# Graph network layer on one core: part of the x rows gathered by GpSimd beside the chunk loop, 21 chunks of counts instead of 25

## The reference

```python
msg = x[src] + edge_attr                                  # 206250 x 128
agg = segment_sum(msg, dst, num_segments=6250)            # 6250 x 128
h = relu(agg @ W1 + b1) @ W2 + b2                         # 128 -> 256 -> 128
h = (h - mean(h)) * rsqrt(var(h) + 1e-5) * ln_w + ln_b    # over all of h
sub = h - gn_ms * mean(h, axis=0)
h = sub * rsqrt(mean(sub ** 2, axis=0) + 1e-5) * gn_w + gn_b
out = layernorm(x + gelu(h) + x)                          # 6250 x 128
```

## Time and profile before

| | us |
|---|---|
| median of 3 runs | 906.94 (905.07 to 907.28) |
| profiled execution | 911.31 |
| its span, first to last instruction | 909.3 |
| PE busy | 729.4 (80%) |
| DVE busy | 678.4 (75%) |
| ACT busy | 383.4 (42%) |
| POOL busy | 145.4 (16%) |
| granted TensorE clock, mean | 0.959 |

### The profile page before, as it was taken

One profiled execution on the slowest core, in us unless ns is written; L12 is line 12 of the kernel. 1 busy time (PEld: TensorE's weight loads), 2 busy tenths in 40 slices (PEclk: granted clock), 3 DMA queues, 4 the chain that ended last, 5 costly groups with the idle time before them and its releaser, 6 DMA issues.

```text
span 909.3 us, 25887 instructions
## 1 busy us (share of the span) xinstructions
PE 729.4 (80%) x9449; PEld 633.5 (70%) x9449; DVE 678.4 (75%) x1185; ACT 383.4 (42%) x841; POOL 145.4 (16%) x91
## 2 busy tenths in 40 slices
PE   3486569888988888988889988889988889989950
PEld 2464448777877777877777877777877777877830
DVE  5844777877878877878877878877878877844576
ACT  0200034355433555433554433554434554424464
POOL 1210022120221220221120221220221220200000
PEclk9987989899999999999999999999999999999975
DMA  6669973443334443334444334443334444303004
GB/s 173 228 216 361 360 262 99 124 147 115 104 100 121 147 144 116 106 97 125 147 144 114 107 94 128 147 144 112 109 93 130 147 144 113 94 25 141 0 1 141
DMA packets 89477, 123.25 MB, mean 136 GB/s; under 512 B 9029, under 2 KB 85018, under 8 KB 89260
## 3 DMA queue, kind: packets, MB, share of 16 engines
q1 hardware_dynamic: 78992, 112.83, 39.9%
q0 software_dynamic: 6240, 5.08, 2.1%
q10 hardware_dynamic: 4228, 5.12, 1.8%
HBM read 118.91 MB, written 4.03 MB: 135 GB/s over the span
## 4 chain that ended last, share of the span: by engine, by line
PE 48%; DVE 26%; issue 11%; DMA 7%; ACT 5%; DVEq 2%; ACTq 1%; POOL 0%; SPq 0%; POOLq 0%
PE bank L693 33%; DVE pool_m L982 12%; DMA edges<-in_edge_attr_dram 5%; PE bank L622 3%; PE bank L672 3%; ACT counts L519 3%; DVE onehot L875 3%; PE bank L740 3%; PE bank L750 2%; PE bank L656 1%; PE bank L636 1%; DMA agg<-in_dst_dram 1%; DMA begins<-listed,tile_slot 1%; DVE node_f L965 1%; DVE node_f L957 1%
## 5 line engine op out<-in xcount | busy, mean ns | idle before, releaser
L519 ACT CAST counts<-bank 128x490 fp32r<-128x490 f32 x625 | 318.3, 606 | 324.0 <-PE bank L672 324.0
L693 PE MATMUL bank<-counts,x_hi 128*128 128x250 f32 x1225 | 293.5, 284 | 29.6 <-ACT counts L519 29.6
L693 PE MATMUL bank<-counts,x_lo 128*128 128x250 f32 x1225 | 290.6, 281 | 0.0
L982 DVE TENSOR_TENSOR pool_m<-listing,turned_lo 128x3328 bf16<-128x3328 bf16 x125 | 236.7, 1893 | 30.1 <-PE bank L672 26.7
L693 PEld LDWEIGHTS bank<-counts,x_hi 128*128 128x128 f32 x1225 | 234.8, 192 | 33.4 <-ACT counts L519 33.4
L672 PE MATMUL bank<-pool_m 128*128 128x98 bf16 x3125 | 211.2, 210 | 33.0 <-ACT counts L519 22.7
L693 PEld LDWEIGHTS bank<-counts,x_lo 128*128 128x128 f32 x1225 | 235.2, 192 | 0.0
L672 PEld LDWEIGHTS bank<-pool_m 128*128 128x128 bf16 x3125 | 161.9, 99 | 77.6 <-ACT counts L519 75.2
L982 DVE TENSOR_TENSOR pool_m<-listing,turned_key 128x2548 bf16<-128x2548 bf16 x125 | 184.5, 1476 | 0.0
L622 PE MATMUL bank<-edges,onehot 128*32 128x128 f32 x3228 | 126.7, 293 | 30.1 <-DMA edges<-in_edge_attr_dram 23.3
L429 POOL DMA_INDIRECT begins<-listed,tile_slot x52 | 101.9, 1959 | 297.1 <-DVE tile_slot L935 265.2
(11 more groups left out here) (149 smaller groups left out, 407.9 us busy)
## 6 DMA issues: line engine op xcount, KB each, us to landing
edges<-in_edge_attr_dram SPq DMA_DIRECT2D x134, 768.0 KB, 4.5
out_dram<-pool_m SPq DMA_DIRECT2D x6, 512.0 KB
begins<-listed,tile_slot POOLq DMA_INDIRECT x52, 4.2
agg<-in_dst_dram SPq DMA_DIRECT2D x1, 768.0 KB
agg<-in_src_dram ACTq DMA_DIRECT2D x1, 768.0 KB
listed<-agg ACTq DMA_DIRECT2D x1, 768.0 KB
begins<-listed,row_slot POOLq DMA_INDIRECT x26, 4.3
w<-in_L_gnn_W_dram ACTq DMA_DIRECT2D x2, 128.0 KB, 2.2
```

Source lines behind the costliest of these rows:

```text
L519: nc.scalar.copy(counts[:, :, k * nodes:(k + 1) * nodes].rearrange("p q (i m) -> p q i m", m=PAIR), cps[k % RING][:, 0:nodes * NT].rearran ...
L693: last = nc.tensor.matmul(sps[:, 0:CHUNK], part[:, q, :], counts[:, q, :], start=(q == 0 and part is x_hi), stop=(q == NT - 1 and part is ...
L982: last = dve.tensor_tensor(to[b % MARKED], values[:, :, 0:n, :].to_broadcast([P, BLOCKS_B, n, INTER]), of.to_broadcast([P, BLOCKS_B, n, IN ...
```

## The change

The first 36864 edges (24 units of 1536) are no longer counted. Their x rows are gathered by GpSimd from x in DRAM, 128 rows of 512 bytes with one indirect DMA, 12 for a unit, and PE sums them with the same one-hot tile as the unit's edge attributes. The counts start at node 1000 (`FIRST` = 4 chunks), so 21 chunks are left. Nodes whose edges lie on both sides of edge 36864 get both parts.

- The edges behind the units make 55 full groups and a rest of 426. The lead has 6 rounds instead of 8; three units lie in its last three rounds, one unit in each of the 21 chunks.
- A chunk has on PE, beside its two groups, the 12 matmuls of a unit's edges (after bank 5), 4 matmuls on each of three sections of gathered rows (after banks 11, 17 and 23), and `turn_unit` inside the 98 matmuls. DVE marks, places and adds the unit in `head`, and `stage_row` moves from `rest` into `head`, before the third batch. ACT copies the unit's sums behind the last bank.
- GpSimd stages four indices in a small tile for each section and issues 4 gathers. `begins` is now one DMA of 1 KB rows instead of two of 512 bytes.
- The halves of the groups have three slots instead of four from the fourth round on; the fourth is the unit's.
- In the setup the row loads of dst and src, and the stores of `listed`, are cut otherwise: 32 rows, 23 rows and a rest, instead of 64, 3 and a rest, and 24 rows for the units. The first of them no longer waits for padding. DVE copies the turned dst columns with the written side in order of memory. The weights are loaded after the loop, into tiles that it used.

The diff, cut to its core:

```diff
+UPER = 3
+UNIT = SUBS * USUB            # USUB = P * UPER
+UNITS = 24
+FIRST = 4
+LEAD_UNITS = 3
+UNIT_SLOTS = (0, 1, 3, 1)
+UNIT_EDGES_AT = 5
+SECTIONS_AT = (11, 17, 23)
+UNIT_TURN_Q = 12
...
-            sp.wait_ge(rows_padded, 2)
-            sp.dma_start(rows_i[0:EVEN, :], dst_full[0:EVEN, :]).then_inc(dst_loaded, 16)
+            sp.dma_start(rows_i[0:EVEN, :], dst_full[0:EVEN, :]).then_inc(dst_loaded, 16)
+            sp.wait_ge(units_padded, 1)
+            sp.dma_start(rows_i[UNIT_AT:ROWS_AT, :].rearrange("u (s e) -> u s e", s=SUBS)[:, :, 0:USUB], dst_units
+                         ).then_inc(dst_loaded, 16)
+            sp.wait_ge(rows_padded, 2)
             sp.dma_start(rows_i[EVEN:FULL, :], dst_full[EVEN:FULL, :]).then_inc(dst_loaded, 16)
...
+            def load_unit_round(r):
+                load(r * GPC, 0, 0, 0, r * HPC + 1)
+                load_unit(r - UNIT_FROM)
+                load(r * GPC, 1, 1, 1, r * HPC + HALVES)
+                load(r * GPC + 1, 0, 2, 3, r * HPC + 3)
+                load(r * GPC + 1, 1, 3, 1, r * HPC + (HALVES + 2))
...
-                for k in range(2):
-                    pool.indirect_dma_start(begins[0:PAIRS, k * P:(k + 1) * P], None, listed_rows,
...
+            def gather_section(c, e):
+                if e == SECTIONS - 1:
+                    pool.wait_ge(unit_summed, c + LEAD_UNITS)
+                else:
+                    pool.wait_ge(sections_free, c * (SECTIONS - 1) + (e + 1))
+                pool.tensor_copy(idx_slot[:, e:e + 1, :], unit_idx[:, bass.ds(c + LEAD_UNITS, 1), e * SUBS:(e + 1) * SUBS]
+                                 ).then_inc(idx_staged, 1)
+                pool.wait_ge(idx_staged, c * SECTIONS + (e + 1))
+                pool.sem_inc(gathers_begun, 1)
+                for b in range(SUBS):
+                    pool.indirect_dma_start(unit_rows[:, e, b * D:(b + 1) * D], None, x,
+                                            bass.IndirectOffsetOnAxis(idx_slot[:, e, b:b + 1], 0)
+                                            ).then_inc(rows_gathered[e], 16)
+
+            pool.wait_ge(unit_idx_ready, 1)
+            gather_lead(0, range(0, 6))
+            gather_begins(0)
+            gather_lead(0, range(6, U_TILES))
+            gather_near(0)
+            for u in range(1, LEAD_UNITS):
+                gather_lead(u, range(U_TILES))
+            with pool.Fori(0, CHUNKS) as c:
+                gather_section(c, 0)
+                gather_begins(c + 1)
+                gather_section(c, 1)
+                gather_near(c + 1)
+                gather_section(c, 2)
...
+            def sum_rows(e, rows):
+                for b in range(SUBS):
+                    last = nc.tensor.matmul(unit_ps[b * WINDOW:(b + 1) * WINDOW, :], unit_oh[:, e * SUBS + b, :],
+                                            rows[:, b * D:(b + 1) * D], start=False, stop=(e == UPER - 1),
+                                            skip_group_check=True)
...
+                    if k == UNIT_EDGES_AT:
+                        sum_unit_edges(c + LEAD_UNITS, True)
+                    if k in SECTIONS_AT:
+                        sum_section(c, SECTIONS_AT.index(k))
...
                 for q in range(NT):
+                    if q == UNIT_TURN_Q:
+                        turn_unit(c + LEAD_UNITS)
...
+                base = unit_base(c + (LEAD_UNITS - 1))
+                mark_unit(c + LEAD_UNITS)
+                add_unit(c + (LEAD_UNITS - 1), base, g - 1)
+                put_unit(c + LEAD_UNITS)
                 mark(g, 1, 0)
                 put(g, 0)
+                stage_row(c + 1)
                 mark_batch(c, 2)
```

More of the change, by code:

```diff
@@ L199, in gnn_kernel @@
         ident = sb("ident", [P, P])
-        ones = sb("ones", [P, P])
+        ones = unit_rows[:, 1, 0:P]
         ones_b = sb("ones_b", [P, 1], BF16)
@@ L500, in copy_keys @@
                                    ).then_inc(keys_ready, 1)
-            for g in range(LEAD0 * GPC):
-                copy_sums(g, g % GPC)
-            with act.Fori(LEAD0, LEAD - 2) as r:
+            for r in range(LEAD - 1):
                 round_copies(r)
-            act.wait_ge(pads_ready, 2)
+            act.wait_ge(pads_ready, 1)
             act.wait_ge(keys_turned, 1)
@@ L510, in _ @@
                                ).then_inc(keys_ready, 1)
-            for r in range(LEAD - 2, LEAD):
-                round_copies(r)
+            round_copies(LEAD - 1)
             def copy_chunk(c):
@@ L614, in _, with sum_half @@
                     last.then_inc(turned, 1)
+            pe.wait_ge(unit_src_ready, 1)
+            unit_ident = ident[UNIT_AT:ROWS_AT, UNIT_AT:ROWS_AT]
+            of_dst = rows_f.rearrange("u (s q) -> u s q", s=SUBS)[:, :, 0:USUB].rearrange("u s (p e) -> u s p e", e=UPER)
+            of_src = unit_src.rearrange("u (s p e) -> u s p e", s=SUBS, e=UPER)
+            for bank, of in ((4, of_dst), (5, of_src)):
+                for e in range(UPER):
+                    for b in range(SUBS):
+                        t = e * SUBS + b
+                        last = nc.tensor.transpose(banks[bank][:, t * UNITS:(t + 1) * UNITS], of[UNIT_AT:ROWS_AT, b, :, e],
+                                                   unit_ident)
+                last.then_inc(turned, 1)
             search(range(DST_AT + 1, 2 * SETS))
-            def sum_half(u, s, k, subs=SUBS):
+            def sum_half(u, slot, s, k, subs=SUBS):
                 oh = onehot[:, u % PLACES, :].rearrange("p (j w) -> p j w", w=WINDOW)
@@ L622, in sum_half @@
                         last = nc.tensor.matmul(eps[s][b * WINDOW:(b + 1) * WINDOW, :], oh[:, t, :],
-                                                edges[:, u, t * D:(t + 1) * D], start=(k == 0 and j == 0),
+                                                edges[:, slot, t * D:(t + 1) * D], start=(k == 0 and j == 0),
                                                 stop=(k == 1 and j == PER // 2 - 1), skip_group_check=True)
@@ L659, in _ @@
             turn_keys(0)
-            for r in range(LEAD - 2, LEAD):
-                round_groups(r)
+            round_groups(LEAD - 1)
             def count_chunk(c):
@@ L758, in _ @@
             down(1, 2 * HC, None)
-            with pe.Fori(0, (CHUNKS - 3) // 2) as it:
+            with pe.Fori(0, (MCHUNKS - 3) // 2) as it:
                 for u in range(2):
```

386 lines of the change are left out of this document (263 added, 123 removed).

## The result

The changed kernel takes 1036.16 us (median of 4 runs, 1029.9 to 1052.14), the kernel before 907.11 us (4 runs): 1.139 times as long, 95% interval 1.131 to 1.148. The run of 1052.14 us was a slow one and the ratio leaves it out; the fast runs took 1029.9 to 1042.23 us. 833 us was predicted, with a range up to 864. The profiled execution took 1042.23 us, its span 1040.4 us.

The account below looks back on a forecast made before the run. Lead bound by DMA; chunks by PE's multiplication and a PE, DVE, ACT chain. Loop start 139 + 21 x 28.1 (590.1) + 10 first-chunk excess + 95.9 tail = 835 us span, 833 us median; 822 to 848, wider 800 to 864.

Parts of the forecast that it names:

- Then POOL needs 14 x 1.6 = 22.4 us ... it fits: Chunk loop: 14 gathers at 1.6 us plus staging copies take GpSimd some 25.5 us of a 28.1 us chunk.
- the bounds (1.5 to 2.27 us): Chunk loop: GpSimd's time for one gather, low beside short VectorE instructions, high from the mean of 1.97 with 0.30.
- These are 61 us, then 4.2 to landing ... 72 us after the clear: Lead: 36 gathers, `begins` and `near` at 1.6 us, landing, then about 6.5 us of halves before the loop starts.
- the 139 predicted: Loop start: clear ending at 67.5 us plus 72 us gives 139.5 us, 20 us later than before.
- Additions on PE and DVE: Chunk loop: a unit's matmuls and `turn_unit` add 0.8 us, making 28.1 us; DVE's additions fit its 2.9 us wait.
- the low bound: Chunk loop: PE's additions add only 0.2 us a chunk, if only half of `turn_unit` shows.
- the excess of the first chunks: Start of the loop: the first chunks' clock and late `begins` cost 10 us beyond the regular chunks.
- The setup: Before the lead: 23-row pieces on one DMA engine delay dst and src to about 33 us, the clear to 67.5.
- GpSimd becomes the bound and the kernel slower: Rival, chance 0.08: in the loop gathers wait out several DVE instructions; 2.27 us each gives 974 us, slower from 2.05.
- my cases: Whole kernel: own sum 0.40, costless 23 rows 0.16, cheaper lead 0.14, PE or POOL late 0.17, GpSimd bound 0.08.
- What would show it: Signs in the profile, among them lead gathers 1.5 to 1.7 us apart, loop start near 139, chunks of 28.1 us.
- chunks over 29.5 us: Chunk loop: a sign that would make the forecast wrong upwards, against 28.1 us expected.

Follow-up runs that it names:

- the ninth: The changed kernel without the units' gathers, its 23-row pieces of dst, src and listed rows cut into 16 and 7: 803.14 us.
- fourth: The changed kernel with GpSimd waiting before each unit gather until the gather two before it has landed: 942.14 us.
- eighth: The changed kernel with 16 one-column memsets on GpSimd behind each gather of a unit: 935.21 us.
- thirteenth: The kernel before with 12 more gathers a chunk, each followed by 16 memsets on GpSimd: 1051.2 us.
- fourteenth: The changed kernel, 16 memsets between a section's gathers, none behind its last in the loop, list's first gather ahead of the units', 23-row pieces cut: 883.18 us, ratio 0.969.
- fifteenth: The changed kernel, 12 memsets between a section's gathers, none behind its last in the loop, list's first gather ahead of the units', 23-row pieces cut: 876.83 us, ratio 0.961.

## Why the prediction was wrong

- **Step that failed: "Then POOL needs 14 x 1.6 = 22.4 us ... it fits".** I asked only whether GpSimd has the time, not what its gathers do to the others. It has the time: 1.22 us a gather, and it waited 120.9 us in all for TensorE to free the sections. But 12 gathers cost the rest 9.0 us a chunk, 189.4 us in the loop: stops of all engines, and a multiplication that partly runs at the lower granted clock after one (1.9 us of the 9.0 on average, 3.0 in the chunk shown). The sum had no term for either. The kernel before never had more than two in a row, so no row could show it; and the bounds (1.5 to 2.27 us) were of GpSimd's time only.
- **The lead.** "These are 61 us, then 4.2 to landing ... 72 us after the clear" took the gathers as work beside the rest. Without any, the loop starts 67.8 us after the clear (138.4 against 70.6): the rest of the lead alone takes as long as I gave the gathers. That the kernel without gathers starts at 138.4, as the 139 predicted, is luck, and the gathers put 39 to 43 us on it (181.0 and 177.7 against 138.4).
- **Additions on PE and DVE.** +0.8 us predicted, nothing measured (27.4 with them against 27.5 before). They hide among the banks, as the low bound had it (0.2), and so does `turn_unit`. 21 x 0.7 = 15 us too dear; with the excess of the first chunks at some 4 us instead of 10 this is why the kernel without gathers takes 815 and not 833 us.
- **The setup.** Right, within about 3 us: first use at 36.1 (33 predicted), clear ended at 70.0 (67.5), a DMA share of 0.06 to 0.07 from 25 to 35 us, and cut pieces bring both back (the ninth). The Trainium skill (DMA: Bandwidth & Descriptors, Why a DMA increments its semaphore by 16 and not by 1) gives the reason, that a DMA runs on the largest number of engines up to 16 that divides its outer sizes; the ninth agrees with 16 and 7 rows in place of 23.
- **Rivals.** The second, "GpSimd becomes the bound and the kernel slower", had the sign and the place, at 0.08, but not the mechanism: its gather of 2.05 us was not reached. GpSimd led the chain only in the fourth, eighth, thirteenth, fourteenth and fifteenth experiments, where the spacing was bought with waits or memsets. None of my cases held that a free engine's DMAs slow the others.
- **"What would show it"** worked: chunks over 29.5 us and lead gathers 1.25 instead of 1.5 to 1.7 us apart were the two signs. The second is telling. I expected VectorE's instructions to keep the gathers 1.6 us apart, and at that distance they would have been harmless to the others (the eighth and fourteenth). Once the others stand, nothing keeps the gathers apart, and they come at 1.25, so that the stop feeds itself (read from the traces, not tested by a run of its own).

What stays open: what the gathers and the other engines' issue share. It is not the rows read, their number, the bytes or the DMA packets. After the lead's last gather the others stand 5.7 us more, as if something were worked off, but no view shows what. How long a run must be for a stop was not measured by itself. For five in a row the bound in spacing lies between 1.41 and 1.52 us here, with 1.45 nearly free; whether it moves with other work beside it was not tried.

## What to carry to other kernels

Work that goes to an idle engine is not free because that engine has room: ask what it issues, and try the densest run of it once beside the others (here 12 gathers added to the old kernel) before building on it. In this kernel runs of indirect DMAs on GpSimd had to be at least 1.5 us apart on average. A few small instructions between them ended the stops and brought 1036 us to 935; it took fewer of them, the cut pieces (11.5 us) and the list's gather ahead of the units' to get to 0.961 times the time before. Chain entries of "issue" and "unknown queue" that appear on several engines at once point to something shared, not to any of them.

## What the runs showed of the hardware

- Runs of indirect DMAs 1.25 us apart stop the other engines together: in the lead TensorE gets 50 matmuls through in 42 us instead of 439, VectorE stands for 46.4 us, ScalarE for 42.1, SyncE for 41.0. Plain DMAs of GpSimd with the same 64 KB, issued 0.55 us apart, do nothing of the kind (910.87 against 908.72 us).
- A gather of 32 rows takes GpSimd 0.88 us, one of 128 rows 0.94, with 0.30 between two: the cost is the gather's.
- In the chunk shown TensorE stood without a matmul for 4.1 us; then its granted clock was 0.50 for 7.7 us of work, and 0.99 after that.
